# A ternary feed-forward stage: convolution taps read from PSUM, one rounding pass, four tiles transposed together

## What is computed

```python
def act_quant(x):
    scale = 127.0 / jnp.clip(jnp.max(jnp.abs(x), axis=-1, keepdims=True), 1e-05)
    return jnp.clip(jnp.round(x * scale), -128, 127) / scale
def weight_quant(w):
    scale = 1.0 / jnp.clip(jnp.mean(jnp.abs(w)), 1e-05)
    return jnp.clip(jnp.round(w * scale), -1, 1) / scale
h = bit_linear(x, w1)                                   # (4, 512, 1024), quantised x and w1
h = depthwise_conv1d(h.transpose(0, 2, 1), conv_w, conv_b)  # 3 taps over the tokens, zero padded
h = jax.nn.silu(h.transpose(0, 2, 1))
return bit_linear(h, w2)                                # quantised h and w2
x = x + _L0_ffn_ref(_layernorm(x, axis=-1), ...)
x = x + _L1_attn_ref(_layernorm(x, axis=-1), ...)
```

## Time and profile before

| | |
|---|---|
| median of three executions | 2282.96 us (2278.29 to 2286.14) |
| the profiled execution | 2282.62 us, its span 2280.8 us |
| mean granted TensorE clock | 0.977 of full |
| PE, DVE, ACT, POOL busy | 88%, 78%, 59%, 9% of the span |

### The profile page before, as it was taken

One profiled execution on the slowest core, in us unless ns is written; L12 is line 12 of the kernel. 1 busy time (PEld: TensorE's weight loads), 2 busy tenths in 40 slices (PEclk: granted clock), 3 DMA queues, 4 the chain that ended last, 5 costly groups with the idle time before them and its releaser, 6 DMA issues.

```text
span 2280.8 us, 43223 instructions
## 1 busy us (share of the span) xinstructions
PE 2013.3 (88%) x18002; PEld 1135.7 (50%) x18002; DVE 1771.3 (78%) x2767; ACT 1342.1 (59%) x1997; POOL 206.9 (9%) x215
## 2 busy tenths in 40 slices
PE   2899978889989997989899998798998999788988
PEld 1566653323656773242466666333255676433325
DVE  7787888695778877779587887869867788786956
ACT  3466646477356654748636664565944666455682
POOL 2000001141000000114000000101400000011220
PEclk9999989999999998999999999899999999989999
DMA  6267720010037670002006765001001767400100
GB/s 256 42 123 121 127 54 1 1 75 29 18 74 121 124 130 19 2 1 94 11 19 105 126 125 111 1 2 74 21 10 40 121 124 124 76 1 2 75 2 10
DMA packets 417315, 147.68 MB, mean 65 GB/s; under 512 B 404440, under 2 KB 412768, under 8 KB 416224
## 3 DMA queue, kind: packets, MB, share of 16 engines
q1 hardware_dynamic: 416544, 142.82, 30.2%
q0 software_dynamic: 576, 2.10, 0.3%
HBM read 41.86 MB, written 2.10 MB: 19 GB/s over the span
## 4 chain that ended last, share of the span: by engine, by line
PE 52%; DVE 27%; DMA 8%; issue 6%; ACT 6%; POOL 1%; SPq 0%; POOLq 0%; DVEq 0%; ACTq 0%
DVE nmx L1857 10%; PE ps L577 10%; PE ps L579 9%; PE ps L578 9%; DMA arena<-arena 7%; PE ps L923 4%; PE ps L739 3%; PE ps L965 2%; DVE arena L1656 2%; PE ps L909 2%; PE ps L733 2%; PE ps L734 2%; PE ps L877 2%; DVE arena L1801 1%; PE ps L597 1%
## 5 line engine op out<-in xcount | busy, mean ns | idle before, releaser
L1857 DVE TENSOR_REDUCE nmx<-ps 128x2 f32<-128x1024 f32 x384 | 443.8, 1218 | 19.7 <-PE ps L877 17.8
L1364 ACT ACTIVATE arena<-ps 128x512 f32<-128x512 f32 x768 | 405.6, 602 | 54.4 <-PE ps L909 49.8
L577 PE MATMUL ps<-arena 128*128 128x512 f16 (+1 forms) x800 | 274.5, 343 | 3.5 <-DVE arena L1997 2.7
L578 PE MATMUL ps<-arena 128*128 128x512 f16 (+1 forms) x800 | 274.5, 343 | 0.0
L579 PE MATMUL ps<-arena 128*128 128x512 f16 (+1 forms) x800 | 274.1, 343 | 0.0
L1643 DVE TENSOR_SCALAR_CACHE_REDUCE ps<-ps 128x1536 f32<-128x1536 f32 x128 | 225.8, 1764 | 48.6 <-PE ps L579 48.0
L923 PE MATMUL ps<-arena 128*17 128x256 f32 x3072 | 237.9, 386 | 0.0
L1656 DVE SCALAR_TENSOR_TENSOR arena<-arena,rs 128x1536 f16<-128x1536 f32 x128 | 231.6, 1810 | 4.2 <-ACT arena L1257 4.2
L1257 ACT ACTIVATE arena<-arena,rs 128x1536 f16<-128x1536 f32 x128 | 200.8, 1568 | 40.1 <-DVE rs L1649 40.1
L1250 ACT ACTIVATE arena<-ps,nm 128x1536 f32<-128x1536 f32 x128 | 197.1, 1540 | 15.2 <-DVE ps L1643 15.2
L733 PE MATMUL ps<-arena 128*128 128x128 f16 x1536 | 185.3, 219 | 2.7 <-DMA arena<-arena 2.7
(11 more groups left out here) (262 smaller groups left out, 3835.5 us busy)
## 6 DMA issues: line engine op xcount, KB each, us to landing
arena<-in_experts SPq DMA_DIRECT2D x4, 3840.0 KB, 11.6
arena<-in_weights SPq DMA_DIRECT2D x8, 929.0 KB, 12.6
arena<-in_ctx SPq DMA_DIRECT2D x4, 1024.0 KB, 5.5
arena<-arena SPq DMA_TRANSPOSE x256, 3.7
arena<-in_ctx_t SPq DMA_DIRECT2D x4, 1024.0 KB, 4.8
arena<-in_ternary SPq DMA_DIRECT2D x2, 1024.0 KB, 5.8
y<-in_x POOLq DMA_DIRECT2D x4, 512.0 KB, 5.1
x<-in_x SPq DMA_DIRECT2D x4, 512.0 KB, 3.7
```

Of the source, the lines that this page charges most:

```text
L577: mm(out_, lh, rh, start=(k == 0), stop=False)
L578: mm(out_, lh, rl_, start=False, stop=False)
L1364: A(pr_[:, n % RING, :], ps[:, 4 + n % 3, :], ACT.Exp).then_inc(b_exp.sem, 1)
L1857: V.tensor_reduce(nmx[:, g_ % 2, ch, :, pp, i], ps[:, 2 * (z % 2):2 * (z % 2) + 2, :], AX.X, ALU.max, negate=True)\
```

## The change

**Convolution.** The padded rows `hp` and the rows for single taps are gone; `conv` has four rows (HB = 4), one for each of the last four `m`, and the matmuls go round four banks (`H_BANK`). ACT writes the middle tap and the bias of `m` into `conv` straight from PSUM; DVE adds the tap before (`before_tap`) and the tap after (`after_tap`), both with the matmul's bank in PSUM as their source. The factor `mw` is multiplied into the tap weights once, at the start of the program (`taps`). PE waits for the tap work of `m-4`, no longer for ACT's copy of `m-2`.

**Tail.** `quantise` has one operation where it had two: the clip is gone. `scales` has one small operation less, and `row_scales` no longer waits for its last one; `add_tile` waits for it. Tiles 2 and 3 are transposed into banks 0 to 3, the convolution's, right behind tiles 0 and 1. ACT takes `scaled(2)` after the first copy from `gq_t`, not before it. BN_AGGR of the first three tiles stands ahead of the last `add_tile`, that of the last tile alone behind it.

**Entry of self attention.** `keep_warm(6, 4)` becomes `keep_warm(3, 4)`, and the third `self_product` stands ahead of `select_k`.

```diff
@@ banks
+        H_BANK = (2, 3, 0, 1)
+        G_BANK = (4, 6, 0, 2)
+        GQ_BANK, F_BANK = (4, 5), (6, 7)
@@ PE bitnet
                 for m in range(NM):
-                    if m >= 2:
-                        pe.wait_ge(h_pad.sem, h_pad.at(b, m - 1))
+                    if m >= HB:
+                        pe.wait_ge(h_conv.sem, h_conv.at(b, m - HB + 1))
...
+                pe.wait_ge(h_conv.sem, h_conv.at(b, NM))
                 for i in range(2, NT):
-                    pe.wait_ge(g_scaled.sem, g_scaled.at(b, i - 1))
                     for m in range(NM):
-                        last = nc.tensor.transpose(ps[:, 4 + 2 * (i % 2) + m // 4, P * (m % 4):P * (m % 4) + P],
+                        last = nc.tensor.transpose(ps[:, G_BANK[i] + m // 4, P * (m % 4):P * (m % 4) + P],
                                                    g[:, m, P * i:P * i + P], ident[:])
@@ PE self_attention
-                keep_warm(6, 4)
+                keep_warm(3, 4)
                 self_product(b, 0)
                 self_product(b, 1)
+                self_product(b, 2)
                 select_k(b, 0, 0)
-                self_product(b, 2)
                 select_q(b, 0, 0)
@@ ACT bitnet
-                    if m >= 3:
-                        act.wait_ge(h_conv.sem, h_conv.at(b, m - 2))
-                    A(hp[:, m % 3, 1:1 + S], ps[:, 2 + m % 2, :], ACT.Copy, scale=mw[:, 0:1]).then_inc(h_pad.sem, 1)
+                    A(conv[:, m % HB, :], ps[:, H_BANK[m % HB], :], ACT.Identity, bias=C("cb", m), scale=taps[:, 3 * m + 1:3 * m + 2])\
+                        .then_inc(h_mid.sem, 1)
...
-                for i in range(3):
+                for i in range(2):
                     scaled(i)
                 for j in range(NT):
                     act.wait_ge(gq_t.sem, gq_t.at(b, j + 1))
...
-                    if j + 3 < NT:
-                        scaled(j + 3)
+                    if j + 2 < NT:
+                        scaled(j + 2)
@@ DVE scales, bitnet
-                own.link(TS_(am, am, 1e-5, None, ALU.max))
-                own.link(V.reciprocal(ri, am))
-                ins = TS_(sc, ri, 127.0, None, ALU.mult)
+                own.link(TS_(ri, am, 1e-5, 1.0 / 127.0, ALU.max, ALU.mult))
+                ins = V.reciprocal(sc, ri)
...
+                def before_tap(m):
+
+                    dve.wait_ge(h_mid.sem, h_mid.at(b, m + 1))
+                    dst = conv[:, m % HB, 1:S]
+                    own.mark(STT(dst, ps[:, H_BANK[m % HB], 0:S - 1], taps[:, 3 * m:3 * m + 1], dst, ALU.mult, ALU.add))
+
+                def after_tap(m):
+
+                    dst = conv[:, m % HB, 0:S - 1]
+                    STT(dst, ps[:, H_BANK[m % HB], 1:S], taps[:, 3 * m + 2:3 * m + 3], dst, ALU.mult, ALU.add).then_inc(h_conv.sem, 1)
+
+                for m in range(NM + 1):
+                    if m < NM:
+                        before_tap(m)
+                    if m:
+                        own.wait(1 if m < NM else 0)
+                        after_tap(m - 1)
...
-                    own.mark(TS_(gt[:, q, :], gt[:, q, :], ROUND, -128.0, ALU.subtract, ALU.max))
                     if i >= 2:
                         dve.wait_ge(gq_t.sem, gq_t.at(b, i - 1))
-                    own.wait()
-                    TS_(gi[:, q, :], gt[:, q, :], 127.0, None, ALU.min).then_inc(g_quant.sem, 1)
+                    TS_(gi[:, q, :], gt[:, q, :], ROUND, None, ALU.subtract).then_inc(g_quant.sem, 1)
```

More of the change, by code:

```diff
@@ L148, in decoder @@
         msc = sb("msc", [P, 2])
+        taps = sb("taps", [P, 3 * NM])
         nm = sb("nm", [P, 8])
@@ L224, in decoder @@
         lay = Layout()
-        hp = lay.take([3, S + 2])
-        conv = lay.take([2, 3, S])
+        conv = lay.take([HB, S])
         g = lay.take([NM, S])
@@ L1487, in stats, with aggregate, moments @@
                 own.mark(V.bn_stats(st[:, i, :], src[:, i, :]))
-            def moments(b, k, src, first=0, twice=False):
+            def aggregate(i):
+                own.mark(V.bn_aggr(mv[:, i, :], st[:, i, :]))
+            def moments(b, k, src, first=0, twice=False, left=0):
                 for i in range(first, NT):
@@ L1494, in moments @@
                 own.wait()
-                for i in range(NT):
-                    own.mark(V.bn_aggr(mv[:, i, :], st[:, i, :]))
+                for i in range(left, NT):
+                    aggregate(i)
                 own.wait()
@@ L1788, in bitnet @@
                 split_lo(b, 1, yT)
-                for k in range(3):
-                    own.mark(V.memset(hp[:, k, 0:1], 0.0))
-                    own.mark(V.memset(hp[:, k, 1 + S:2 + S], 0.0))
-                own.wait()
-                def tap(m, k):
-                    src, dst = hp[:, m % 3, k:k + S], conv[:, m % 2, k, :]
-                    if k == 0:
-                        dve.wait_ge(h_pad.sem, h_pad.at(b, m + 1))
-                        own.mark(TS_(dst, src, C("cw", 3 * m), C("cb", m), ALU.mult, ALU.add))
-                        return
-                    ins = STT(dst, src, C("cw", 3 * m + k), conv[:, m % 2, k - 1, :], ALU.mult, ALU.add)
-                    if k == 1:
-                        own.mark(ins)
-                    else:
-                        ins.then_inc(h_conv.sem, 1)
@@ L1845, in bitnet @@
                 quantise(NT - 1)
-                for j in range(1, NT + 1):
-                    if j < NT:
-                        add_tile(j, ivs[j])
-                    dve.wait_ge(f_added.sem, f_added.at(b, j))
-                    stats(x, j - 1)
+                for j in range(1, NT):
+                    add_tile(j, ivs[j])
+                    if j < NT - 1:
+                        dve.wait_ge(f_added.sem, f_added.at(b, j))
+                        stats(x, j - 1)
+                    if j == NT - 2:
+                        dve.wait_ge(f_added.sem, f_added.at(b, j + 1))
+                        stats(x, j)
+                        own.wait()
+                        for i in range(NT - 1):
+                            aggregate(i)
+                dve.wait_ge(f_added.sem, f_added.at(b, NT))
+                stats(x, NT - 1)
             def max_slot(b, mode, a):
@@ L1966, in self_attention @@
             def self_attention(b):
-                norm(b, 2, x, y, NT)
+                moments(b, 2, x, NT, left=NT - 1)
+                normalise(b, 2, x, y)
                 split_lo(b, 2, yT)
@@ L2052, in _ @@
                 TS_(dst, src, 1.0, None, ALU.mult).then_inc(sel_set.sem, 1)
+            dve.wait_ge(const_in.sem, 16 * 5)
+            own.mark(TS_(taps[:], col[:, COL["cw"]:COL["cw"] + 3 * NM], mw[:, 0:1], None, ALU.mult))
             pad = ident[:].rearrange("p (e n) -> p e n", e=2)[:, :, HR:SR]
```

48 lines of the change are left out of this document (20 added, 28 removed).

## The result

| | before | after |
|---|---|---|
| median, beside each other on one chip | 2281.99 us (4 runs) | 2255.24 us (2249.72 to 2255.92, 4 runs) |
| profiled execution, its span | 2282.62, 2280.8 | 2255.41, 2253.6 |
| mean granted TensorE clock | 0.977 | 0.983 |

The ratio is 0.9883, 95% interval [0.9867, 0.9898]: 1.2% faster. The forecast was 2253, range 2245 to 2265.

A forecast was written before the change was run, and what follows sets the result against it. The prediction took a chain of waits, mostly on DVE, to bound the ternary block. Convolution 2.9, tail 3.5 and entry 1.0 made 7.4 us a sequence, times 4 = 29.6 off 2282.6: 2253 us, range 2245 to 2265.

The forecast's parts named there:

- The bound: Ternary block: a chain of waits mostly on DVE, where a microsecond taken out is one of the kernel, four times over.
- Taps from PSUM: Convolution: DVE's two-input taps take the same from PSUM as from SBUF, holding DVE 0.66 us, 0.75 to their end.
- The ring of 1.44 to 1.46 us a group: Convolution: DVE's taps, ACT's Silu and middle tap take 2.87 us for two groups, 1.44 each; 1.46 with PE's part.
- The convolution: First tap to the tail's first maximum: 2.9 us less a sequence, bounds 2.3 and 3.4.
- The tail: First maximum to variance: 4.2 us less at full clock or 1.0 less at half; 3.5 taken.
- The layout for full clock: Tail: with PE at full clock, first maximum to variance takes 14.0 us, where it was 18.24.
- My lower bound, 17.3 with half clock to the end: Tail: with PE at half clock, PE is the bound and first maximum to variance takes 17.3 us, 1.0 less.
- nearer to full clock, since before it was the earlier part of the tail that ran at half clock: Tail: the reason given for taking 3.5 us, between 4.2 less at full clock and 1.0 at half.
- The sign I had named, a wait for PE before the last add: Tail: a wait of 0.5 us or more on DVE was to show the forecast right.
- The entry: Entry of self attention: fewer keep_warm and the reordered product bring select_q forward; 1.0 us a sequence, bounds 0.5 to 1.7.
- The half clock: Rival: PE falls to half clock mid-tail and stays, the entry runs at half clock too; 2265 us, chance 0.17.
- The other two rivals: Convolution: ACT or PE still binds at 1.78 us a group, 2263, chance 0.06; PSUM-sourced taps slow, 2294, chance 0.04.

The follow-up runs named there:

- old_conv: The kernel after with the convolution of before put back (padded rows in SBUF, three taps, two banks); 2268.89 us, ratio 0.994.
- no_bias: The kernel after with the convolution's bias left out, so ACT's middle tap is shorter; first tap to first maximum 12.38 us for 12.56 in three sequences.
- warm_both: The kernel after with unread matmuls in two PE gaps: seven in the tail, ten before the wait for the variance; 2246.65 us, ratio 0.9846.
- old_entry: The kernel after with six keep_warm and the third self_product between the two selections again; 2260.73 us, ratio 0.9913.
- warm_entry: The kernel after with ten unread matmuls between the tail's last product and the wait for the variance; 2256.94 us, ratio 0.989.
- warm_tail: The kernel after with seven unread matmuls behind the tail's first eight transposes back; 2254.26 us, ratio 0.9877.
- warm_all: warm_both with four more unread matmuls behind the transposes in front of the convolution; 2252.36 us, ratio 0.9884.

## Why the prediction was right, step by step

**The bound.** Right: 27.4 us came out of the stage, 27.2 out of the time. That parts add along one chain is shown by undoing each: by the stage the convolution is worth 9.8, the second pass 8.0, the banks 5.2, the small operations 3.4, the entry 2.7, the moved BN_AGGR 0.8, together 29.9 for 27.4. The total came closer than its terms: the convolution gave 1.7 us more than forecast over the four sequences, tail and entry together 4.1 less, so part of the nearness of 2253 to 2255.24 is luck.

**Taps from PSUM.** Right. The tap before takes 748 ns and the tap after 741, against 746 and 747 ns in the earlier trace rows. The grouped lines after:

```profile
L1800 DVE SCALAR_TENSOR_TENSOR arena<-ps,taps,arena 128x511 f32<-128x511 f32 x32 | 23.9, 748 | 7.8 <-ACT arena L1326 6.3
...
L1326 ACT ACTIVATE arena<-ps,col,taps 128x512 f32<-128x512 f32 x32 | 24.7, 773 | 7.6 <-PE ps L836 6.4
```

The Trainium skill ("VectorE: DVE Perf Modes", section "Rules for kernel authors") offers two ways, to accept the slowest mode of a PSUM source or to copy to SBUF first if many operations follow. Here two operations from PSUM beat the copy with three from SBUF by 12.8 us in the convolution's piece (old_conv). That is not because PSUM is the better source: the two-input form takes the same from either, and the gain is the third operation, which moved from DVE into the one that ACT made anyway, for 773 ns there in place of 678.

**The ring of 1.44 to 1.46 us a group.** Right, 1.446, and no_bias shows that a ring through ACT sets it; the trace's own chain has the ring with PE in it, for which the forecast said 1.46. The convolution was mis-sized at its ends: the first tap did not start 0.1 later (2.59 us after the split of y for 2.57), the way to the last group's first tap is 9.41 us, not 9.6, and from the last group's first tap it is 0.8 us less, not 0.65. In sum 3.3 for 2.9.

**The tail.** The layout for full clock was right: 14.0 us forecast from first maximum to variance, 14.12 measured where the clock stays up (warm_both). The uneven term was the clock. I took 3.5 of 4.2 us; it came to 2.8, because in every sequence the clock was at half for some of the pairs. My lower bound, 17.3 with half clock to the end, never occurred; the worst tail of this code was 16.06. Wrong in its reason was "nearer to full clock, since before it was the earlier part of the tail that ran at half clock": before, that cost nothing as DVE covered it, and the change took that cover away. The sign I had named, a wait for PE before the last add, did not come: the three BN_AGGR fill it. The wait is at the second and third adds.

**The entry.** I took 1.0 us a sequence; measured 0.67. The first sequence gives 1.5, but there the kernel before ran part of its entry at half clock (granted clock 0.59 from 348 to 350 us and 0.56 to 352) and the kernel after none. With full clock on both sides the edit is worth 0.73 (old_entry). So the term was mis-sized by itself, apart from the clock, and in the way that the forecast had put at its lower bound: with three `keep_warm` fewer, PE waits for `yT_lo`. At full clock, counted from the variance, the first product starts 0.56 us earlier but the second only 0.30, and `select_q` about 0.75. The clock costs the entry about the same before and after: the mean before is 11.72 us, 0.74 above its full-clock 10.98, the mean after 11.05, 0.81 above 10.24. warm_entry, where it stays up, has 10.24 or 10.25 each time.

**The rivals.** The half clock was the real one, in part: against the kernels that keep it up, it took 15.4 - 14.1 = 1.3 us of the tail and (44.2 - 41.0) / 4 = 0.8 of the entry from each sequence, 8 us in all. Of these the 0.8 had been there before, so what the change paid back is the tail's, about 5 us. One sign that I had named for being wrong came with it: in the first sequence the last tile's eight transposes back took 0.95 us. The other two rivals are refuted by the tap rows and by old_conv.

## What to carry to other kernels

Before cutting an engine's work, look at what this work hides. Here PE's half clock cost nothing in the tail while DVE was the bound, and began to cost 5 us there when DVE was relieved. Where a stage repeats in one execution, compare its repetitions: equal to 0.01 us, the engine that is busy throughout sets the pace; uneven, look at the clock and at transfers first. And measure such a stage between two fixed instructions: its edits of 2 to 5 us were clear there and hard to tell in a total whose other parts differ by 13 us from one kernel's execution to another's.

## What the runs showed of the hardware that I had not expected

The same seven matmuls in the tail left it at 15.4 to 15.5 us in five sequences and at 14.1 to 14.4 in seven (warm_tail, warm_both, warm_all), mean 14.7 against 15.5 us over the sixteen sequences of after, old_entry, warm_entry and no_bias, which lack them. What sets the five and the seven apart is when the clock had fallen before. In the seven it fell between 1.7 us before the first maximum and 0.4 behind it, came back within 3.8 us of the maximum (5.2 in one), and then stayed up. In the sequences without the seven matmuls where it fell so and came back so, it fell a second time 6.1 to 7.1 us after the first maximum (four of four), and the tail took 14.8 to 15.1 us. In the five, the clock was full at the first maximum and fell 4.3 to 4.9 us behind it; it was back 3.4 us later, where it took 6.8 us without the matmuls. So they held the clock in the one case and shortened the half-clock stretch in the other; no run sets the moment of the first fall by itself. The kernel's code doesn't fix that, so the same code of the tail has several times, 14.78 to 16.06 us, and warm_both's 57.8 for warm_tail's 62.0 is a matter of which case its sequences met.
